# Spreading, clearing and batch order in a recommendation tower: two ids ahead, late padding, two batches beside each pack

## The reference

```python
# D = 128; B = 512 samples; 26 tables of 1000 to 125000 rows of 128 floats
e = jnp.stack([tbl_f[ids[:, f]] for f in range(26)], axis=1)  # written out table by table
T = jnp.concatenate([dense[:, None, :], embs], axis=1)      # 27 features
Z = jnp.einsum('bnd,bmd->bnm', T, T)
iu0, iu1 = jnp.triu_indices(N, k=1)
return Z[:, iu0, iu1]                                       # 351 products a sample
...
h = jnp.concatenate([z, r_dense], axis=1)                   # 479 columns
h = jnp.maximum(h @ W_top1 + b_top1, 0.0)                   # 479 x 512
h = jnp.maximum(h @ W_top2 + b_top2, 0.0)                   # 512 x 256
y = h @ W_top3                                              # 256 x 1
```

## Time and profile before

| | us |
|---|---|
| median of the runs | 136.8 |
| lowest, highest | 136.19, 136.98 |
| the profiled execution's own time | 137.93 |
| its span, first to last instruction | 136.1 |

### The profile page before, as it was taken

The page is one execution under the profiler, slowest core; times in us unless marked ns, Lnnn a source line. Parts: engine busy times, 40 slices in busy tenths (PEclk is TensorE's granted clock), DMA queues, the critical chain, the costliest instruction groups (busy, mean ns, idle before and its releaser), DMA issues. The chain is left out here.

```text
span 136.1 us, 2673 instructions
## 1 busy us (share of the span) xinstructions
PE 118.9 (87%) x1008; PEld 96.7 (71%) x1008; DVE 85.1 (62%) x211; ACT 70.5 (52%) x133; POOL 64.8 (48%) x63
## 2 busy tenths in 40 slices
PE   5799999999999999999944529995993998799994
PEld 5474678767778778888942319774893998797991
DVE  4499829956889999999205005285608529982221
ACT  3490458589596947653551008438826336752212
POOL 3978878477848887887777725550000000000000
PEclk9999999999999999999998555698569999999999
DMA  3951899999666476437221210200000000000000
GB/s 102 287 143 39 207 238 234 208 209 214 128 194 199 91 205 197 110 126 193 58 58 45 57 39 19 58 24 19 0 0 5 2 5 0 5 0 0 5 0 0
DMA packets 5098, 12.67 MB, mean 93 GB/s; under 512 B 2039, under 2 KB 2166, under 8 KB 5086
## 3 DMA queue, kind: packets, MB, share of 16 engines
q1 hardware_dynamic: 2996, 8.46, 24.3%
q0 software_dynamic: 1792, 3.67, 11.7%
q10 hardware_dynamic: 298, 0.37, 0.8%
HBM read 12.50 MB, written 0.00 MB: 92 GB/s over the span
## 5 line engine op out<-in xcount | busy, mean ns | idle before, releaser
L373 POOL DMA_INDIRECT rows<-tbl,idx_sb x56 | 64.0, 1143 | 25.8 <-issue 10.1
L617 PE MATMUL sums<-onehot,table_h 125*128 125x512 f32 (+1 forms) x105 | 41.0, 394 | 0.0
L499 DVE TENSOR_SCALAR onehot<-ids_rel 125x512 fp32r<-125x512 f32 x108 | 38.6, 427 | 2.1 <-ACT ids_rel L411 1.7
L619 PE MATMUL sums<-onehot,table_l 125*128 125x512 f32 (+1 forms) x105 | 39.6, 381 | 0.0
L662 PE MATMUL gram<-featT 128*64 128x52 f32 x512 | 20.1, 235 | 4.2 <-issue 4.1
L617 PEld LDWEIGHTS sums<-onehot,table_h 125*128 125x128 f32 x105 | 19.7, 188 | 5.6 <-issue 1.9
L432 ACT COPY featT<-sums 128x512 f32<-128x512 f32 (+1 forms) x12 | 12.6, 1053 | 20.8 <-PE sums L619 17.5
L662 PEld LDWEIGHTS gram<-featT 128*64 128x64 f32 x512 | 18.3, 150 | 6.9 <-issue 6.8
L619 PEld LDWEIGHTS sums<-onehot,table_l 125*128 125x128 f32 x105 | 19.7, 188 | 3.7 <-issue 0.2
L385 DVE COPY products<-gram 32x208 f32<-32x208 f32 x32 | 12.0, 376 | 14.5 <-remote 7.8
L491 DVE TENSOR_TENSOR table_l<-raw,table_h 125x1280 fp32r<-125x1280 f32 (+2 forms) x12 | 15.8, 1316 | 6.0 <-PE sums L619 4.4
(11 more groups left out here) (66 smaller groups left out, 122.7 us busy)
## 6 DMA issues: line engine op xcount, KB each, us to landing
raw<-tbl SPq DMA_DIRECT2D x6, 560.0 KB
raw<-tbl SPq DMA_DIRECT2D x5, 448.0 KB
raw<-w SPq DMA_DIRECT2D x3, 512.0 KB
rows<-tbl,idx_sb POOLq DMA_INDIRECT x56
raw<-tbl SPq DMA_DIRECT2D x6, 65.0 KB
raw<-tbl ACTq DMA_DIRECT2D x1, 280.0 KB
raw<-tbl SPq DMA_DIRECT2D x5, 52.0 KB
denseT<-dense_t SPq DMA_DIRECT2D x1, 256.0 KB
```

The lines of the kernel that those rows point to most:

```text
L373: pool.indirect_dma_start(rows[:, t % 2, s, :], None, tables[f], bass.IndirectOffsetOnAxis(ap=idx_sb[:, t, f:f + 1], axis=0)).then_inc(row ...
L499: nc.vector.tensor_scalar(onehot[0:SELECT_PARTS, n % ONEHOTS, :], ids_rel[0:SELECT_PARTS, k % IDS_BUFFERS, :], float(c), None, ALU.is_equa ...
L617: nc.tensor.matmul(dst, table_h[0:SELECT_PARTS, n % PART_BUFFERS, c, :], hot, start=(c == 0), stop=False)
L619: nc.tensor.matmul(dst, table_l[0:SELECT_PARTS, n % PART_BUFFERS, c, :], hot, start=False, stop=(c == PLACES[n] - 1)).then_inc(chunk_selec ...
```

## The change

Five edits. The spreads ahead of the selection are two, not four, and the warm-up products behind them two, not four; the third and fourth spread stand ahead of select 1, and from select 2 on one spread stands ahead of each select, two tables ahead. The clearing of the padding moves from VectorE's start to behind its last one-hots. In the order of steps each pack has two product batches beside it (P2[0] and P2[1] at pack 1, P3[0] and P3[1] at pack 2), the dense columns of the second pair move from behind layer 2 of the first pair to ahead of `pairsT` 2. The warm-up products at the end go from three and two to none and one. Layer 2's matmuls run one output half at a time within a bank, and the low parts of both banks are taken with the second bank, each half with its own wait.

```diff
--- before.py
+++ after.py
@@ -73,7 +73,7 @@
 DENSE_CHUNK = PAIR_CHUNKS
 CHUNKS1 = PAIR_CHUNKS + 1
 
-WARM_UP_PRODUCTS = 5, 4
+WARM_UP_PRODUCTS = 5, 2
 ONEHOTS = 12
 IDS_BUFFERS = 3
 
@@ -127,13 +127,15 @@
 
 
 
-    order = [("keep_warm", WARM_UP_PRODUCTS[0])] + [("spread_ids", k) for k in range(SPREAD_BANKS)]
+    order = [("keep_warm", WARM_UP_PRODUCTS[0])] + [("spread_ids", k) for k in range(AHEAD)]
     order.append(("keep_warm", WARM_UP_PRODUCTS[1]))
     for k in range(SELECTED_COUNT):
         if k == 4:
             order.append(("dense_high", 0))
-        if SPREAD_BANKS <= k + 3 < SELECTED_COUNT:
-            order.append(("spread_ids", k + 3))
+        if k == 1:
+            order.append(("spread_ids", AHEAD))
+        if 1 <= k < SELECTED_COUNT - AHEAD:
+            order.append(("spread_ids", k + AHEAD))
         order += [("select", k), ("rows", 1 if k >= ROWS_BEHIND else 0)]
 
     P0, P1, P2, P3 = ([("products", BATCHES * t + n) for n in range(BATCHES)] for t in range(TILES))
@@ -146,12 +148,12 @@
         P1[1], ("pack_act", 0), ("weights_in", 2), row, ("pairsT", 0),
         P1[2], ("dense", 0), row,
         P1[3], ("pack", 1),
-        P2[0], ("pack_act", 1), ("pairsT", 1),
-        P2[1], ("layer1", 0),
-        P2[2], P2[3], ("pack", 2),
-        P3[0], ("pack_act", 2), P3[1], ("pairsT", 2),
-        P3[2], P3[3], ("pack", 3), ("pack_act", 3), ("layer2", 0), ("dense", 1),
-        ("pairsT", 3), ("scores", 0), ("layer1", 1), ("keep_warm", 3), ("layer2", 1), ("keep_warm", 2), ("scores", 1),
+        P2[0], ("pack_act", 1), P2[1], ("pairsT", 1),
+        P2[2], ("layer1", 0),
+        P2[3], ("pack", 2),
+        P3[0], ("pack_act", 2), P3[1], ("dense", 1), ("pairsT", 2),
+        P3[2], P3[3], ("pack", 3), ("pack_act", 3), ("layer2", 0),
+        ("pairsT", 3), ("scores", 0), ("layer1", 1), ("layer2", 1), ("keep_warm", 1), ("scores", 1),
     ]
     group = 0
     for step, n in order:
@@ -505,8 +507,6 @@
             nc.vector.memset(packed[:, :, BIAS_AT:BIAS_AT + 1], 1.0).then_inc(packed_set, 1)
             dve.wait_ge(identity_ready, 1)
             nc.vector.tensor_copy(ones_at[:], identity[0:SELECTED_COUNT, 0:SELECTED_COUNT]).then_inc(ones_ready, 1)
-            nc.vector.memset(featT[:].rearrange("p t g b s -> p (t g b) s")[:, :, FEATURES:SLOTS], 0.0
-                             ).then_inc(padding_set, 1)
             dve.wait_ge(ids_rows_landed, 16)
             nc.vector.tensor_copy(ids_rows_r[:], ids_rows[:]).then_inc(ids_rows_ready, 1)
             for step, n in SCHEDULE:
@@ -521,6 +521,9 @@
                         load_in(n + 1)
                     if n >= 1:
                         build_onehots(n, range(middle, PLACES[n]))
+                    if n == SELECTED_COUNT - 1:
+                        nc.vector.memset(featT[:].rearrange("p t g b s -> p (t g b) s")[:, :, FEATURES:SLOTS], 0.0
+                                         ).then_inc(padding_set, 1)
                 elif step == "dense_low":
                     dve.wait_ge(dense_high, 1)
                     nc.vector.tensor_tensor(dense_l[:], denseT[:], dense_h[:].bitcast(fp32),
@@ -717,18 +720,17 @@
                     pe.wait_ge(pairs_low, pairs_begun)
                     for g in range(BANKS1):
                         units = range(BLOCKS * g, BLOCKS * (g + 1))
-                        pe.wait_ge(h1_high, BANKS1 * n + g + 1)
-                        for u in units:
-                            for o in range(N2):
+                        for o in range(N2):
+                            pe.wait_ge(h1_high, BANKS1 * n + g + 1)
+                            for u in units:
                                 for w in (w2_h, w2_l):
                                     nc.tensor.matmul(hidden2(o), w[:, u, P * o:P * (o + 1)], h1T_h[:, u, :],
                                                      start=(u == 0 and w is w2_h), stop=False)
-                        pe.wait_ge(h1_low, BANKS1 * n + g + 1)
-                        for o in range(N2):
-                            for u in units:
-                                last = nc.tensor.matmul(hidden2(o), w2_h[:, u, P * o:P * (o + 1)], h1T_l[:, u, :],
-                                                        start=False, stop=(u == N1 - 1))
                             if g == BANKS1 - 1:
+                                pe.wait_ge(h1_low, BANKS1 * (n + 1))
+                                for u in range(N1):
+                                    last = nc.tensor.matmul(hidden2(o), w2_h[:, u, P * o:P * (o + 1)], h1T_l[:, u, :],
+                                                            start=False, stop=(u == N1 - 1))
                                 last.then_inc(h2_summed, 1)
                     layers2_done = n + 1
                 elif step == "scores":
```

## The result

The changed kernel takes **133.67 us** (median of 6 runs, 130.52 to 135.09), the kernel before 137.0 beside it. That is 3.3 us by the medians. Ratios in this document, given with their 95% intervals, compare only the runs within 1.5% of each kernel's fastest: here it is 0.958 (0.950 to 0.966), so 5.8 us. Forecast were 2.4. What was not foreseen either is the spread: 4.6 us between runs of one program. The profiled execution took 135.09 us, its span 133.3 (before 136.1).

What follows compares the result with a forecast made beforehand. TensorE was taken as the bound in the selection (12.2 to 68 us), with one dependent chain from 111.3 us on. Start 0.6 plus end 1.9 make 2.5, with hand-overs 2.4 us: 134.4 us at the median's level, range 132.4 to 137.0.

Steps and rivals of the forecast that it cites:

- The selection's start: Kernel start: fewer spreads and warm-up products, no early clearing; selection begins at 5.95 instead of 8.70, 2.75 us earlier.
- The wait behind select 0: In select 1: TensorE waits 1.3 us behind the late third spread; select 1 ends 1.6 us later against that spread.
- The clearing: Padding memset moved behind VectorE's last one-hots: 2.19 us, ending at 67.8, hidden by 1.5 us before the first products.
- (c): Late clearing holds up the gathers and the hold follows: run ends 1.6 us later, 136.0 us; chance 0.08.
- The change leaves the stretch from 68 to 103 us as it is.: Middle of the kernel, with the hold: nothing changes there but for the clearing.
- Batches beside the packs: Two product batches beside each pack, so pack 2 and its turning come 0.78 us earlier.
- Dense columns: Dense 1 gone from behind layer 2: turning of pack 3 starts at 121.98 instead of 123.23, 1.25 us gained so far.
- Warm-up products and layer 2's order: Kernel end: 0.6 us from three products removed, 0.15 from one more, less 0.1 for the second bank's late low part.
- (a): Clock falls in the new wait in select 1, costing 3.4 us in the selection: 137.8 us; chance 0.10.
- (b): At the selection's start the clock does not rise sooner than 12.1 us: 135.8 us; chance 0.12.
- (d): Hold tied to a place in TensorE's instruction stream; missing it gives 126, partly 130 to 132 us; chance 0.08.
- (e): The end gives nothing, its steps waiting elsewhere, and the start gives nothing either: 136.8 us; chance 0.12.

Runs made afterwards that it cites:

- gate 48: The changed kernel with GATHERS_IN_SELECTION 48 in place of 50, so gathers 48 and 49 wait for the first product batch: 132.48 us, ratio 0.973 to the kernel before.
- the end alone: The kernel before with only the order of steps from P2[0] on and layer 2's loops changed: 134.06 us, ratio 0.984 to the kernel before.

## Why the prediction was right and wrong

The two profiles of one batch (before and changed, beside gate 48) give the accounts: 134.3 before, 129.1 changed, 5.2 us. Of these 2.4 lie ahead of the first batch (80.0 to 77.6), 1.7 between first and last batch (37.15 to 35.43), 1.05 behind the last (17.13 to 16.08). The first batch's median of 133.67 lies inside the stated 132.4 to 137.0 and 0.7 us from the forecast, which is in part luck, since its profiled run holds the stalled gather; by the ratio the kernel would stand at 131.0 beside the 136.8 of the forecast, outside the range, with more than twice the gain that was summed. In the five batches of runs with a hold the gain is 2.6 to 4.2 us by the medians and 3.3 to 5.8 by the ratios. The parts that were summed (0.6 and 1.9) do not reach it, for a term was put at nothing: what the clearing's old place cost.

**The selection's start.** Said 2.75 us sooner and a start at 5.95; it was 2.45 and 6.25. The cast of ids began at 2.49, sooner than the 2.7 that was said, but TensorE began the spreads at 4.06 in place of 3.9 and the warm-up products behind them 1.14 us later in place of 1.0. The clock rose at 10.63 in place of 12.09, so 1.5 us sooner for a start that came 2.45 sooner: between the two bounds. In the other profiles with the changed start it rose between 8.3 and 11.6, so this term scatters more than it was bounded. At the next spread (13.46, before 15.37) 1.9 us were left.

**The wait behind select 0.** Said 1.3 us, behind VectorE's load of table 2; from one matmul's start to the next it is 1.46 us in the first profile and 1.42 to 1.43 in all others with this order (0.23 without a wait, so 1.2 of waiting), and the load ends 0.4 us ahead of its end. Selection 2 then starts 0.3 us sooner than before, and the selection's last matmul 0.1 later: the start's own sum of 0.6 us came out as nothing at the selection's end. In the pair of one batch that matmul is 2.1 us sooner (67.20 and 69.29), but 2.0 of it is one wait of the kernel before, at 36 us, that its first profile doesn't have. The selection's end scatters by as much as the start could win.

**The clearing** was said to be hidden behind the last one-hots, and so it was: it ends at 68.20, and the first products wait for ScalarE's copy at 70.04, which ends at 70.63. The step that failed is the other half of that sentence, that it costs and gives nothing else. **The first gather's 2.65 us were in the earlier trace rows, and were put down to the gather's being the first**, in rival (c), which looked at them for a loss only: it asked what the clearing does where it comes to, not what it did where it came from. With it in its old place the first gather takes 2.64 to 2.75 us in four profiles of four, in place of the 1.10 without, and put back there it has the run of gathers end 2.4 us later, the first batch 1.9 and the kernel 1.6 (0.2 to 3.0). Where it came to, the gather beside it took 0.94 us. So (c) had the mechanism (the hold ends with the gathers) and the opposite sign. (It read 2.4 us from the last gather's end to the hold's; from 79.13 to 81.66 it is 2.5.)
The Trainium skill, "SBUF — State Buffer", practical consequences, says that a VectorE instruction with at most one SBUF input outside the two-port modes does not contend with GpSimd, which would cover a memset. The gather of 0.94 us beside the late clearing agrees. The early one speaks against it without settling it: in all four profiles that gather begins at 2.9 to 3.0 and ends at 5.68, 1.25 us behind the clearing's end and 0.97 behind that of the ids' cast that follows (4.36 to 4.71). At 1.10 us it would have ended before that cast began, so the clearing is the nearer suspect; no run here has the one without the other.

**"The change leaves the stretch from 68 to 103 us as it is."** This carried the forecast and was wrong. The hold is not a stretch of fixed place. It ends with the run of gathers, and the time at the low clock is 10 to 17 us in the five profiles of the changed kernel in place of 17 to 20 in the two of the kernel before. Of the 1.7 us between the first batch and the last, the batches beside the packs account for 0.8. The 0.9 that are left may be the clock's, which is argued and not shown: behind the first batch the kernel before has 12.2 us at the low clock in that pair, the changed one 6.7. What sets the time at the low clock was not tested by itself.

**The end** is right term by term. Batches beside the packs: said 0.78; from the ninth batch, P2[0], to the last it is 15.01 us in place of 15.78, so 0.77. Dense columns: they end before the turning at 114.68 and the turning of pack 3 stands 3.77 us behind the last batch in place of 4.24, 0.47 for 0.47. Warm-up products and layer 2's order: 0.58 for 0.65, and the wait for the low part inside it, at 128.37, is 0.15 for 0.1. Sum 1.8 for 1.9; the end alone, timed, 1.7 by the medians and 2.2 by the ratio.

**The rivals.** (a) No: the new wait of 1.2 us and the one of 1.1 us for pack 1 left the clock at 1.00. (b) In part, 10.63 in the first profile. (d) Fell: without the last gathers the code comes at nearly the same matmul (326th and 329th) and nothing is held.
By the Trainium skill, "Runtime: NRT & Kernel Launch", instruction fetch mechanics, code comes in blocks ahead of use; that run agrees, the packet at 71.9 us delays nothing. (e) No.

What stays open: why TensorE's posts are held at all, why they were not in one batch of runs, what stalls a gather for 3.16 us, and what the hold is besides late posts: TensorE's matmuls are slow in it as well. At the end of the first profile's hold they start one every 0.7 us (78.58, 79.30, 80.02, 80.71, 81.43), and the same steps run without a pause where nothing is held.

## What to carry to other kernels

Ahead of a resource that works through one long queue (here GpSimd's 50 gathers), a delay of its first item can come out at the end of the last: price an edit not only by who waits for the moved instruction, but by what ran beside it in its old place. A stretch that no engine's work explains has a cause that may move; find what ends it (here the last gather of a run) before calling it constant. And take a second profile of one program before reading a difference: two of the changed kernel differed here by 3 us in the very place that decided.

## What the runs showed of the hardware

TensorE's completions can be held while GpSimd issues indirect gathers back to back: in the first profile of the changed kernel none was posted from 71.44 to 81.54 us, and then seven within 0.3 us, though 24 matmuls started in that time; in the 14 other profiles with a hold it is 7.3 to 12.2 us, and seven posts again. The hold was absent without the last tile's gathers, ended 1.4 to 2.5 us behind the last one of the run with them, and was absent with them in both profiles of one batch of runs that could show it; the kernel before took 128.3 there in place of 135.3 to 137.2. Four gathers later in the kernel, issued back to back, were enough for a shorter one (83.07 to 88.64 with gate 48). A gather that took 3.16 us in place of 1.10 moved the end of a 133 us kernel by 2.8 us.
